# Cross-attention and mixture of experts on one core: 11 expert slots run beside the last group's routing, from a first slot table

## What is computed

```
x = x + tanh(g_xattn) * (softmax(q k^T / 8) v @ Wo + bo)      q from layernorm(x), k and v from ctx
xn = layernorm(layernorm(x)) * gamma + beta
probs = softmax(xn @ router_w.T);  topk_p, topk_i = top_k(probs, 2)
for e in range(8):
    xe = xn * dense_gate[:, e]
    gate, up = split(xe @ gate_up_w[e].T)
    out += (silu(gate) * up) @ down_w[e].T
x = x + tanh(g_ffn) * (layernorm(x) + out)
```

## Time and profile before

| | us |
|---|---|
| median of 3 runs | 585.88 (584.28 to 585.99) |
| the profiled execution, its own time | 591.32 |
| its span | 589.5 |
| PE busy | 519.3 (88%) |
| DVE busy | 339.2 (58%) |
| ACT busy | 283.5 (48%) |
| POOL busy | 233.9 (40%) |

### The profile page before, as it was taken

The page is one execution under the profiler, slowest core; times in us unless marked ns, Lnnn a source line. Parts: engine busy times, 40 slices in busy tenths (PEclk is TensorE's granted clock), DMA queues, the critical chain, the costliest instruction groups (busy, mean ns, idle before and its releaser), DMA issues.

```text
span 589.5 us, 12387 instructions
## 1 busy us (share of the span) xinstructions
PE 519.3 (88%) x3712; PEld 478.6 (81%) x3713; DVE 339.2 (58%) x783; ACT 283.5 (48%) x866; POOL 233.9 (40%) x319
## 2 busy tenths in 40 slices
PE   7999999999999998999998840299999999999991
PEld 6789999998899898998988740178888888888881
DVE  5856666668677577774756567245555555533330
ACT  3446565665555555554655102245555555544330
POOL 5160000329006782057730843314434544443332
PEclk8999999999999999999999865589999999999997
DMA  8500000000000201002010396555565556333322
GB/s 246 190 1 2 0 2 1 20 1 9 29 2 0 71 0 36 0 1 73 2 37 0 102 255 200 173 149 117 126 160 125 118 132 160 54 53 53 55 37 28
DMA packets 32500, 41.54 MB, mean 70 GB/s; under 512 B 3216, under 2 KB 28560, under 8 KB 32464
## 3 DMA queue, kind: packets, MB, share of 16 engines
q1 hardware_dynamic: 25312, 31.75, 18.2%
q0 software_dynamic: 7152, 9.33, 10.1%
HBM read 24.12 MB, written 16.95 MB: 70 GB/s over the span
## 4 chain that ended last, share of the span: by engine, by line
PE 59%; DVE 12%; ACT 8%; issue 6%; DMA 6%; DVEq 3%; SPq 2%; POOL 2%; another core or an unknown queue 1%; POOLq 0%; ACTq 0%
PE bank L1288 17%; PE bank L1308 9%; PE bank L610 7%; PE bank L588 6%; ACT probs L780 5%; PE bank L550 4%; PE bank L534 4%; PE bank L564 3%; PE bank L1298 3%; DVE nmax L899 2%; DMA expert_queue<-zrow 2%; DMA out_dram<-yq,to_row 2%; PE bank L713 2%; PE bank L1271 1%; DVEq L909 1%
## 5 line engine op out<-in xcount | busy, mean ns | idle before, releaser
L780 ACT ACTIVATE probs<-bank,nmax 128x154 f32<-128x154 f32 x256 | 97.6, 388 | 123.4 <-DVE nmax L899 119.2
L588 PE MATMUL bank<-vdiag,pT 128*128 128x128 f32 (+2 forms) x640 | 80.7, 273 | 7.0 <-DVE oT_lo L923 6.9
L588 PEld LDWEIGHTS bank<-vdiag,pT 128*128 128x128 f32 (+1 forms) x640 | 78.3, 193 | 10.4 <-DVE oT_lo L923 10.3
L1243 POOL DMA_INDIRECT out_dram<-yq,to_row x39 | 60.8, 1559 | 33.7 <-issue 24.1
L1288 PE MATMUL bank<-gu_hi,xqT_hi 128*128 x156 | 69.0, 442 | 1.1 <-DVE xqT_lo L1405 1.1
L1412 DVE TENSOR_TENSOR hid<-hid,bank 128x512 f32<-128x512 f32 x39 | 26.8, 688 | 66.2 <-PE bank L1288 66.2
L899 DVE TENSOR_REDUCE nmax<-bank 128x2 f32<-128x308 f32 x128 | 60.0, 470 | 7.6 <-PE bank L550 6.8
L1288 PE MATMUL bank<-gu_hi,xqT_lo 128*128 x156 | 62.7, 402 | 0.0
L1288 PE MATMUL bank<-gu_lo,xqT_hi 128*128 x156 | 62.0, 397 | 0.0
L564 PE MATMUL bank<-ident,probs 128*128 128x128 f32 (+1 forms) x320 | 46.9, 275 | 5.6 <-ACT xfT L793 2.9
L780 ACT ACTIVATION_READ_ACCUMULATOR probs<-bank,nmax 128x1 f32 x256 | 51.0, 199 | 0.0
(11 more groups left out here) (183 smaller groups left out, 1423.7 us busy)
## 6 DMA issues: line engine op xcount, KB each, us to landing
gu_raw<-in_gate_up_wT_dram SPq DMA_DIRECT2D x16, 512.0 KB
expert_queue<-zrow SPq DMA_DIRECT2D x8, 642.5 KB
xq<-expert_queue SPq DMA_DIRECT2D x39, 128.5 KB
dn_raw<-in_down_wT_dram SPq DMA_DIRECT2D x8, 512.0 KB
x<-in_x_dram SPq DMA_DIRECT2D x4, 512.0 KB, 12.8
out_dram<-out SPq DMA_DIRECT2D x8, 256.0 KB, 2.2
wq_raw<-in_L_xattn_Wq_dram SPq DMA_DIRECT2D x1, 1024.0 KB, 11.4
wo_raw<-in_L_xattn_Wo_dram SPq DMA_DIRECT2D x1, 1024.0 KB, 11.6
```

What stands on the lines that cost most here:

```text
L588: last = nc.tensor.matmul(at[:, col0 + j0 * DH:col0 + j0 * DH + n], pT[u % 2][0:rows, b, :], v, start=(b == 0), stop=(b == NBLK - 1), skip ...
L780: last = nc.scalar.activation(probs[u % 4][:, j * NKB:(j + 1) * NKB], S_BANK[hf][:, m * NKB:(m + 1) * NKB], ACT.Exp, bias=nmax[:, u % 4, j ...
L1243: nc.gpsimd.indirect_dma_start(out[:, :], bass.IndirectOffsetOnAxis(to_row[:, 0:1], 0), yq[p % 2][:, :], None, compute_op=ALU.add).then_in ...
```

## The change

The expert stage moves into the attention block: one program for each engine, with no seam between the stages.

- **Two tables.** After 12 token tiles are routed, `rank_experts` orders the experts by their counts, and `first_table` fills slots 0 to NA - 1 = 10 with tiles that are already full. `count_tiles` and `fill_slots(NA, MT - NA)` fill the other 28 after the last group is counted.
- **A lead expert.** In slot 6 of the last group `find_lead` takes the expert with most rows after 8 token tiles. Its weights are loaded and split in attention's last slots, and slots 0 and 1 run on its first two tiles.
- **The last group's routing** is threaded through expert slots 1 to 8: `first_norm(1)` and `norm_stats` in 1, `second_norm(1)` in 2, features turned in 2 and 3, logits in 3 and 4, the router's exponential at the end of ACT's slot 4, `router_probs` and `choose(0)` in 5, `choose(1)` in 6, counting, row numbers, pad positions and the two output tiles in 7, the second table in 8. POOL sends the rows between scatter-adds 5 and 6.
- **Pads** are 1 tile behind each expert instead of 5, and SP writes them ahead of the rows of slot 11.
- **Weights.** Slots 1 to 23 are written out. `SPLITS` says behind which slot which part of which rank is split, `LOADS` when it is loaded, `NEEDED` at which slot PE waits for it.
- **Buffers.** The gate and up results have one PSUM bank each instead of two; `xn` has one buffer; the SBUF tensors are laid out anew, so that raw weights can land while attention runs, with ranks in falling order. The token numbers have 8 small tiles in the written out slots.
- The gated rows of the third group are made by ACT in slot 14 instead of by POOL.

```diff
-    FIRST_CHUNKS = [(), (0,), (1, 2), ()]
+    NA = 11
+    SENDS = 6
+    COUNT_SLOT = 7
+    UNROLLED = 24
+    NEEDED = {0: 0, 2: 1, 5: 2, 7: 3, 9: 4, 15: 5, 18: 6, 21: 7}
+    SPLITS = {0: ((1, 0), (1, 1)), 1: ((1, 2),), 2: ((2, 0),), 3: ((2, 1),), 4: ((2, 2),), 5: ((3, 0), (3, 1)), 6: ((3, 2),),
+              7: ((4, 0), (4, 1)), 8: ((4, 2),), 12: ((5, 0),), 13: ((5, 1),), 14: ((5, 2),), 15: ((6, 0),), 16: ((6, 1),), 17: ((6, 2),),
+              18: ((7, 0),), 19: ((7, 1),), 20: ((7, 2),)}
...
-        G_BANK, U_BANK, XT_BANK, HT_BANK, Y_BANK = bank[0:2], bank[2:4], bank[4], bank[5], bank[6:8]
+        G_BANK, U_BANK, XT_BANK, HT_BANK, Y_BANK = bank[0], bank[1], bank[6], bank[4], (bank[5], bank[7])
...
+                sp.wait_ge(s["table_a"], 1)
+                sp.wait_ge(s["rows_q"], 16 * 2 * (NT - TPI))
+                for j in range(UNROLLED):
+                    if j + 2 == NA:
+
+                        send_output(NI - 1)
+                        sp.wait_ge(s["pads"], 1)
+                        for e in range(E):
+                            first = sp.value_load(pad[0:1, e:e + 1], min_val=0, max_val=DUMMY - P)
+                            sp.dma_start(queue[bass.ds(first, P), :], zrow[:, :]).then_inc(s["pads_q"], 16)
+                        sp.wait_ge(s["table"], 1)
+                        sp.wait_ge(s["rows_q"], 16 * 2 * NT)
+                        sp.wait_ge(s["pads_q"], 16 * E)
+                        sp.wait_ge(s["out0_q"], 32 * NI)
+                        sp.wait_ge(s["zero_q"], 32)
+                    load_rows(sp, *divmod(j + 2, RT))
...
+                for j in range(SENDS):
+                    slot(*divmod(j, RT))
+
+                pool.wait_ge(s["gated"], 2)
+                tokens(*divmod(SENDS + 2, RT))
+                send_rows(NI, 0)
+                tokens(*divmod(SENDS + 3, RT))
+                send_rows(NI, 1)
+                tokens(*divmod(SENDS + 4, RT))
+                scatter_add(*divmod(SENDS, RT))
...
+                def expert_slot(i, p, more=True):
+
+                    j = RT * i + p
+                    static = isinstance(j, int)
+                    if static and j in NEEDED:
+                        pe.wait_ge(s["w_lo"], 3 * (NEEDED[j] + 1))
...
+                attend(NI, -1, waits=True)
+                transpose_out(NI, 0)
+                pe.wait_ge(s["w_lo"], 2)
+                pe.wait_ge(s["exp"][0], UPI * NI)
+                up(0, 0, 0, 0, G_BANK, "e_gate", "e_silu")
                 transpose_out(NI, 2)
+                transpose_rows(0, 1)
+                pe.wait_ge(s["exp"][1], UPI * NI)
+                up(0, 0, 0, 1, U_BANK, "e_up", "e_hid")
...
+                def expert_slot(i, p, more=True):
+                    j = RT * i + p
+                    static = isinstance(j, int)
+                    hidden_T(*((i - 1, RT - 1) if p == 0 else (i, p - 1)))
+                    if static and j == 1:
+                        split_low(dve, *SPLITS[0][1])
+                        first_norm(1)
+                        norm_stats(NI, 1)
+                    if static and j == 6:
+                        choose(NI, 1)
+                    gated(i, p)
+                    if more:
+                        rows_T(i + (p + 1) // RT, (p + 1) % RT)
+                    if static and j == 2:
+                        second_norm(1)
+                    if static:
+                        for part in SPLITS.get(j, ()):
+                            split_low(dve, *part)
+                    if static and j == 4:
+                        clamped_logits(NI, TA)
+                        shifted_logits(NI)
+                    if static and j == 5:
+                        router_probs(NI)
+                        choose(NI, 0)
+                    if static and j == COUNT_SLOT:
+                        count_rows(NI)
+                        number_rows(NI)
+                        then(v.tensor_tensor(padf[:, :], base_cnt[:, :], region0[:, 0, :], ALU.add))
+                        then(v.tensor_copy(pad[:, :], padf[:, :])).then_inc(s["pads"], 1)
+                        start_output(NI, 0)
+                        start_output(NI, 1)
+                    if static and j == COUNT_SLOT + 1:
+                        count_tiles()
+                        then(fill_slots(NA, MT - NA)).then_inc(s["table"], 1)
...
+                    if u == 6:
+                        find_lead()
+                    if u in (10, 11):
+                        split_low(dve, 0, u - 10)
+                    if u == 13:
+                        first_norm(0)
+                        norm_stats(NI, 0)
+                    if u == 14:
+                        split_low(dve, 0, 2)
+                    if u == 15:
+                        rank_experts()
+                rows_T(0, 0)
                 dve.wait_ge(s["zero"], 1)
...
                 scale_out(NI, -1)
+                transposed_out(NI, 0)
                 block_stats(NI, 2)
...
+                transposed_out(NI, 2)
+                first_table()
+                gated(0, 0)
+                rows_T(0, 1)
+                second_norm(0)
                 add_residual(NI, 3)
```

More of the change, by code:

```diff
@@ L329, in _ @@
+                with sp.Fori(UNROLLED // RT, LOOPS) as i:
+                    for p in range(RT):
+                        load_rows(sp, i + (p + 2) // RT, (p + 2) % RT)
+                for j in range(RT * LOOPS + 2, MT):
+                    load_rows(sp, *divmod(j, RT))
             @block.gpsimd
@@ L753, in _ @@
+                for j in range(RT * LOOPS, MT):
+                    expert_slot(*divmod(j, RT), more=(j < MT - 1))
+                last_tile = divmod(MT - 1, RT)
+                transpose_hidden(*last_tile)
+                down(*last_tile, rank_of(*last_tile))
             @block.scalar
@@ new lines, in gated, with second_features @@
+                def gated(i):
+                    act.wait_ge(s["chosen"], i)
+                    act.wait_ge(s["rows_q"], 16 * 2 * TPI * (i - 1))
+                    for k in range(2):
+                        for j in range(TPI):
+                            last = nc.scalar.activation(rows[:, k, j, 0:D], xf[:, j, :], ACT.Copy, scale=gate[:, k, j:j + 1])
+                    last.then_inc(s["gated"], 1)
+                def second_features():
+                    act.wait_ge(s["xfT_ps"], 2 * NI)
+                    nc.scalar.copy(xfT[:, 4:8, :].rearrange("p c t -> p (c t)"), TB[:, :]).then_inc(s["xfT_sb"][1], 1)
@@ L844, in _ @@
-                for k in range(2):
-                    for j in range(TPI):
-                        last = nc.scalar.activation(rows[:, k, j, 0:D], xf[:, j, :], ACT.Copy, scale=gate[:, k, j:j + 1])
-                last.then_inc(s["gated"], 1)
-                for n in range(2):
-                    split_high(act, 0, n)
+                rows_T(0, 1)
+                for part in SPLITS[0]:
+                    split_high(act, *part)
+                for j in range(1, UNROLLED):
+                    expert_slot(*divmod(j, RT))
@@ L851, in _ @@
+                with act.Fori(UNROLLED // RT, LOOPS) as i:
+                    for p in range(RT):
+                        expert_slot(i, p)
+                for j in range(RT * LOOPS, MT):
+                    expert_slot(*divmod(j, RT), more=(j < MT - 1))
+                hidden_T(*divmod(MT - 1, RT))
+                scaled(*divmod(MT - 1, RT))
             @block.vector
@@ new lines, in first_table @@
+                def first_table():
+                    v.drain()
+                    v.memset(used[:, :], 0.0)
+                    tiles_of(base_cnt, full, 0)
+                    tiles_ahead(full, start_a)
+                    then(v.tensor_copy(start[:, :], start_a[:, :]))
+                    then(v.tensor_tensor(end[:, :], start_a[:, :], full[:, :], ALU.add))
+                    then(fill_slots(0, NA)).then_inc(s["table_a"], 1)
+                    then(v.tensor_scalar(used[:, :], start_a[:, :], -1.0, float(NA), ALU.mult, ALU.add))
+                    then(v.scalar_tensor_tensor(used[:, :], used[:, :], 0.0, full[:, :], ALU.max, ALU.min))
@@ new lines, in count_tiles @@
+                def count_tiles():
+                    then(v.tensor_scalar(cnt1[:, :], base_cnt[:, :], float(P - 1), None, ALU.add))
+                    tiles_of(cnt1, tiles, 1)
+                    then(v.tensor_tensor(left[:, :], tiles[:, :], used[:, :], ALU.subtract))
+                    tiles_ahead(left, start)
+                    then(v.tensor_scalar(start[:, :], start[:, :], float(NA), None, ALU.add))
+                    then(v.tensor_tensor(end[:, :], start[:, :], left[:, :], ALU.add))
```

709 lines of the change are left out of this document (354 added, 355 removed).

## The result

| | before | after |
|---|---|---|
| median, us | 585.08 (583.73 to 585.99) | 594.15 (590.74 to 596.50) |
| the profiled execution, its own time | 591.32 | 590.74 |
| its span | 589.5 | 588.6 |

The ratio after to before is 1.0132, 95% interval 1.0091 to 1.0172. The forecast was 578.0, with a range from 571 to 589. The two profiled executions flatter the change: that of before lies 6.2 us above its own median, that of after is the fastest of its kernel.

What follows compares the result with a forecast made beforehand. Two pacers of nearly equal speed: PE's slots (4.88 us) and POOL's serial scatter-adds (4.95). The walk moved the end from 589.5 to 577.6, clock made it 581.6; 7.9 us gain off the shown median 585.9 gave 578.0, range 571 to 589.

Steps and rivals of the forecast that it cites:

- The walk: Whole changed kernel: engine queues followed in program order with durations from profile rows; span ends at 577.6.
- Slot 2: Third expert slot, after attention: starts at 357.7, 34.7 us before 392.4.
- The term for the delay of attention's last group: Attention's last group: VectorE's added work there delays by 1.5 us, between 0 and 3.
- Slots 2 to 9: Expert slots carrying the last group's routing: VectorE's work makes them uneven, 4.9 to 10.0 us each.
- Slot 10: Expert slot just before slot 11: takes 6.2 us, so slot 11 starts at 421.7 instead of 436.9.
- third rival: Slower: the last group's sends become the bound; sign: PE waits over 2 us for xq at slot 11; 14%.
- Scatter-add 6: On POOL, behind the last group's eight sends: starts at 413.5 instead of 424.4.
- From there 4.96 us: POOL's chain after scatter-add 6: no slack, 32 more at 4.96 us, tile 38 at 572.3.
- Waits for splits: PE waits 1.6 us at slots 5, 15, 18 and 21; POOL's chain hides the waits.
- The clock term: PE's clock falls after pauses, each low stretch costing up to 1.6 us; end taken as 581.6, not 577.6.
- second rival: No change: clock falls after nearly every pause, split waits cost 3.2 us; sign: low clock in slots 15 to 23; 12%.
- The two added table loads: On ACT, router's Exp between two Silu: two more loads, 1.28 us each, at no cost.

Runs made afterwards that it cites:

- e1: The changed kernel run again, unaltered: 592.29 us, ratio 1.0122 to the kernel before.
- e5: The kernel before run again, unaltered, for a second profiled execution: 577.1 us, one execution.
- e4: The kernel before with no drain ahead of the scatter-adds' DMAs, row numbers taken straight from tok: 582.49 us, ratio 0.9984.
- e8: The kernel before with row numbers straight from tok and the drain behind each scatter-add's DMA instead of ahead: 610.39 us, ratio 1.0458.
- e6: The changed kernel with the weight splits of ranks 5 to 7 one slot earlier: 592.41 us, ratio 1.0170.
- e2: The changed kernel with no drain ahead of the scatter-adds' DMAs, row numbers taken straight from tok: 586.96 us, ratio 1.0060.
- e10: The changed kernel without the scatter-adds' drains, splits of ranks 2 to 7 earlier, tile 11's token numbers behind scatter-add 7: 573.72 us, ratio 0.9834.
- e13: As e10, with scatter-add 6 ahead of the sends and one drain put back ahead of the last scatter-add's DMA: 574.03 us, ratio 0.9810.

## Why the prediction was wrong, step by step

**The steps that failed.** The walk took scatter-add 6 at the usual price of its drain and then 32 steps of 4.96 us. The runs showed a pause of 5.35 us ahead of its DMA, and 5.22 us for each of the last 31 steps. The chain's way from slot 2 to the end, by the walk and measured: to scatter-add 6 55.8 and 57.4 us, from there to scatter-add 7 4.96 and 10.1, to the last one 153.8 and 161.9, to the end 5.3 and 5.2, together 219.9 and 234.6 (236.1 in e1).

- **The error of 16.1 us, by parts.** The forecast was an end of the span at 581.6 (the walk's 577.6 and 4.0 for the clock), and it came at 588.6. These 7.0 us are 10.7 too few behind slot 2, less 3.7 by which slot 2 came early. The other 9.1 us lie in how the profile was carried to the median: the forecast took the changed kernel's median 5.4 us below its profile, and it lay 3.4 above. The 5.4 were late attention in one execution (e5), not an offset. So more than half of the error is not the chain's.
- **Slot 2: right by its number, with the help of the profile.** 357.7 forecast, 354.0 and 354.1 measured. But against e4, e5 and e8, whose slot 2 starts at 388.2, 380.7 and 385.4, that is 26.7 to 34.2 us earlier and not 34.7. The term for the delay of attention's last group, 1.5 us with 0 to 3, was too small: the last group got at least 3 us longer.
- **Slots 2 to 9: nearly right.** Forecast 57.8, measured 61.0 (e1: 64.1). Slot by slot in the changed kernel, slots 2 to 9: 5.3, 6.2, 7.9, 4.9, 10.3, 6.7, 9.3 and 10.4 against 5.3, 6.4, 7.4, 4.9, 10.0, 5.3, 9.0 and 9.5. Waits for hidT_lo and for splits came, as said. The walk held no clock, and that is the 3.1 us between the two executions: e1's slots 2 and 5 are 1.6 us longer each, and there, from 355.5 and from 376, its granted clock was 0.50 for some 3.5 us. That a queue of small operations can be walked this closely held.
- **Slot 10: mis-sized, 6.2 against 10.3** (e1: 11.3). Two steps were missing. The pad rows, said to be "done long before slot 11's rows are fetched", were what the fetch waited for: SyncE had issued the last at 412.4 and fetched at 417.98. And ACT waited for scatter-add 6 with everything behind it. From 411 to 417 PE's granted clock was 0.50 besides. PE's wait of 2.6 us for the rows is the third rival's mark, but the pads made it, not the sends.
- **Scatter-add 6: its place was right (413.5; 411.4 measured), its DMA was not.** The drain's cost was read from scatter-adds whose forerunner had landed, where 0.85 us of idle time lie ahead of the DMA and 0.37 of them are the drain; behind the sends it was 5.35. The walk went on at 4.96 at once; scatter-add 7 came 10.1 us later: 5.2 us lost. The rows of before show no drain behind sends under way, so it should have been bounded from both sides, and the landing of a send (2.56 us of DMA in the earlier trace rows) was the upper one to take, though it is half of what came.
- **"From there 4.96 us": failed, 8.1 us in 31 steps.** Of these, 3.6 are four meetings with a split (copies of 1.14 and 1.05 us, issues of 2.33 and 2.55); 4.7 in e1. 2.1 are the late landing of scatter-add 7 beside the loads, and 1.4 one more late landing at 503.9. The prediction had the pairing with a split before it in the earlier trace rows (1.89 us beside a split) and used it for the sends in the third rival, not for the chain, which meets some of the nine late splits once its place in the slot has moved.
- **Waits for splits, 1.6 us each, "hidden" by the chain: half right.** The three late ones measured 2.0 to 2.1, and were hidden indeed (e6). They were the next limit behind the chain (e2).
- **The clock term: not the step that failed.** From slot 2 to slot 11 the granted clock was low for some 14 us in the changed kernel and 19 in e1; by PE's busy time in them this is at most 5.8 and 8.7 us of its work, and the forecast took 4.0. How much of it reached the end no run shows. There was no low clock in slots 15 to 23, so the second rival's mark is missing.
- **The two added table loads** took 1.28 us each (at 371.92 and 374.70), and ACT's next operation stood 0.12 and 0.01 us behind them, as the walk had them.
- **Rivals.** The time came out on the third one's side, but not by its condition (scatter-add 6 after 427.2). Slots further apart than 4.95 us after slot 11 with POOL idle, the last of the marks named, was the right alarm (28 slots in 147.1 us, 5.25 each). The mechanism of the forecast (POOL's chain has no slack, so all depends on where it starts) was right; the walk took the chain at its undisturbed pace. It left out that PE's own waits for splits stood just behind the chain.
- With the chain short and the splits early (e10), the expert stage takes 217.8 us, 2 less than the walk had, and the change with these edits is worth 1.7%. That this is near the 1.3% forecast bears out the head start, not the forecast, which was for the chain as it stood.

## What to carry to other kernels

When a change gives a head start, look at each serial chain that is already at the pace of the bound: it can't make up a pause, and a pause also moves it against its neighbours. Price its step with what it will run beside in the new order, not with its undisturbed median. When two limits are of one height, edits to each alone show little or nothing, and only the pair tells what the change is worth. And look at a second execution before carrying a profile's distance from the median over to another kernel.

## What the runs showed of the hardware

- A drain on GpSimd with indirect DMAs under way is long: 4.4 us in the median from the start of a scatter-add's DMA to the next operation (e8), against 1.03 without the drain (e4); 5.35 us of idle time behind eight sends, against 0.85 with none under way. Whether it waits for the landing itself is not settled: in the changed kernel the DMA engines' share was 0.10 from 414 to 416 and 0.00 from 416 to 418.8, and the DMA behind the drain started at 416.92.
- Over thirty indirect DMAs without a drain leave some 3 us to the next drain or the end, even when all have landed (e13: 3.98 us of idle time; e10: 7.35 us from the start of the last DMA to the end, 4.2 to 4.4 with drains).
- A GpSimd copy of 0.19 us, and the issue of an indirect DMA of 1.55 us, are held by about 1 us when they meet VectorE's subtraction of two SBUF operands; the copy ends when that ends.
- The same kernel's slot 2 started 11.7 us apart in two executions (before and e5), at a granted clock of 0.947 and 0.958 over the span.
